# Reordering the per-chunk schedule of a fused phase mixer and ternary FFN layer, with the ternary comparisons on GpSimd

## The chip, the cores and the metric

The kernel runs on one core of a Trainium2 chip. The metric is the device time of one execution in microseconds; lower is better. Times inside an execution come from one profiled execution, counted from the start of its span.

## The reference

The input x is 16 sequences of 1024 positions and 256 features. Two residual layers follow each other, each on a layer norm of its input.

```python
omega = x @ W_omega.T + b_omega                       # x here: the layer norm of the input
phi = cumsum(omega * exp(log_scale) / sqrt(position), axis=1)
cm_real, cm_imag = x * cos(phi), x * sin(phi)
mem_real, mem_imag = (cumsum(c, axis=1) / position for c in (cm_real, cm_imag))
ret_real = mem_real * cos(phi) + mem_imag * sin(phi)
ret_imag = mem_imag * cos(phi) - mem_real * sin(phi)
h = layernorm(concatenate([cm_real, cm_imag, ret_real, ret_imag])) * gamma + beta
x = x + (gelu(h @ W1.T + b1) @ W2.T + b2)              # added to the mixer's own input and to x
# second layer: weights are ternary, clip(round(W / (mean|W| + EPS)), -1, 1)
out = x + (relu(layernorm(x) @ Wq1.T + b1) @ Wq2.T + b2)
```

## The kernel before, in words

The 16384 rows are cut into 32 chunks of 512; two chunks make a sequence, and the second takes over the running sums of the first. Each engine's stream is written out by hand: a start that works on chunks 0 and 1 and on the weights, and then a function `step`, called once per step s, which works on several chunks at once: `before` (s-1), `now` (s), `nxt` (s+1), `ahead` (s+2) and `far` (s+3). Semaphores carry the dependences (`need` and its kin wait for a chunk's count); within an engine the order is that of the calls, and a waiting instruction holds back all behind it.

What a chunk goes through: `statistics_1` and `normalise_1` (first layer norm), a split of the result in two float16 halves (`first_rows_hi`, `first_rows_lo`), which SP's DMA queue transposes into `turned1`; `omega` (TensorE, L908, 12 matmuls); `phase_turns` (L1193) and the scans `phase_sums` (L1202) on VectorE; `whole_turns` (ScalarE, L608) and `fraction` (L1213) reduce the phase; `sine`, `cosine`; `modulate_imag` and `modulate_real`, the scans `sums_imag` and `sums_real`, division by the position (`memory_imag`, `memory_real`, L1258), the four products of the retrieval, of which `product_imag_sin` (L550) is GpSimd's, and two accumulating DMAs from GpSimd's queue (`retrieve`). Each of the four context parts is split in halves (`context_hi` on ScalarE, `context_lo`, L1291, on VectorE). GpSimd adds the squares (`square_sums`, L534 and L536), and ScalarE takes them over with `sums_hi` (L652). TensorE then makes four hidden blocks (`hidden`, L948, 24 matmuls each) with `context_stats` and `spread` between them; the reciprocal deviations come back by `spread_out` (L662), and `scale_hidden` (L1315), `gelu`, `gelu_hi`, `gelu_lo` follow. `mixer_out` (L999, 48 matmuls) and `mixer_residual` (L1327) end the first layer.

Second layer: `statistics_2`, `spread_2`, GpSimd's `inverse_std_2` (L502), `lean_2`, `normalise_2` (L601), `second_hi`, `second_lo` (L1351); four DMA transposes from SP's queue (L441) give `turned2`. Then eight blocks: `ffn_in(m)` (L965, 4 matmuls of 512 columns), `relu` (L700) and `relu_hi` (L709) on ScalarE, `relu_lo` (L1359) on VectorE, and `ffn_out(m)` (L978, 8 matmuls of 256 columns), which runs three blocks behind. TensorE's order in a step is: hidden 0 and 1, context_stats, hidden 2, spread, hidden 3 (all for `nxt`), the eight input blocks and output blocks 0 to 4 (for `now`), mixer_out (`nxt`), omega (`far`), output blocks 5 to 7 (`now`). `last_mixer` holds the step in which chunk 30 goes through the FFN and chunk 31 through the mixer.

The ternary weights are made at the start. `signs` writes for each of the two matrices two float16 planes, weight above the threshold (L1500) and below its negative (L1501), 128x2048 elements each; TensorE turns them (`turn_signs`), and ScalarE copies them out. VectorE does `signs(0)` and `signs(1)` in step -1. The thresholds (`thr`, L1593 to L1595) are ready late in the part before the steps.

Quoted, the second layer's end of one block and the lag:

```python
for m in range(KF):
    if now:
        ffn_in(now, m, nxt)
        if m >= LAG:
            ffn_out(now, m - LAG)
```

## Time and profile before

| what | value |
| --- | --- |
| median of 3 runs | 1552.74 us (1551.18 to 1555.45) |
| the profiled execution | 1552.36 us, its span 1550.6 us |
| TensorE (PE) busy | 1480.5 us, 95% |
| VectorE (DVE) busy | 1395.3 us, 90% |
| ScalarE (ACT) busy | 1252.0 us, 81% |
| GpSimd (POOL) busy | 583.3 us, 38% |
| DMA | 158.73 MB, mean 102 GB/s |
| mean granted TensorE clock | 0.99 of full speed |

Busy time is a union over an engine's instructions; matmuls overlap each other, and their ends are modelled. The time outside the span, 1.8 us here, belongs to the execution but to no instruction. In the views, "idle before" is the time an engine stood still in front of an instruction, and the arrow names what ended it. PEq, DVEq, ACTq and SPq are the engines' sequencers.

### The profile page before, as it was taken

How to read it: one execution, taken by the hardware profiler on the slowest of the kernel's cores; microseconds unless marked ns; L12 is line 12 of the kernel's file. 1: busy time of each engine (PE TensorE's matmuls, PEld its weight loads, DVE VectorE, ACT ScalarE, POOL GpSimd, SP SyncE). 2: the span in 40 equal slices, each digit the busy share in tenths (PEclk: the TensorE clock that was granted, in tenths of full speed). 3: DMA queues.
4: the chain of work that ended last, by engine and by line, in shares of the span. 5: the costliest groups of instructions: out<-in, count | busy, mean ns of one | idle time of the engine just before them, and what ended most of it. 6: DMA issues, size and time to landing. Idle time of an engine off the chain costs nothing.

```text
span 1550.6 us, 29919 instructions
## 1 busy us (share of the span) xinstructions
PE 1480.5 (95%) x10677; PEld 875.2 (56%) x10677; DVE 1395.3 (90%) x2324; ACT 1252.0 (81%) x1773; POOL 583.3 (38%) x394
## 2 busy tenths in 40 slices
PE   3689999999999999999999999999999999999997
PEld 2355555656555655555565655566555556565564
DVE  6999999999999999999999999999999999999843
ACT  6768888888987888888888897888888888889755
POOL 1323344433344443334443334444333444333421
PEclk9799999999999999999999999999999999999999
DMA  6335655555765645675555567454566555556533
GB/s 217 68 56 110 123 93 100 101 96 104 123 114 88 103 95 94 122 123 93 99 103 96 103 123 119 82 107 95 93 120 123 95 97 103 98 101 109 96 55 55
DMA packets 233603, 158.73 MB, mean 102 GB/s; under 512 B 140784, under 2 KB 223728, under 8 KB 233456
## 3 DMA queue, kind: packets, MB, share of 16 engines
q0 software_dynamic: 59376, 83.37, 34.9%
q1 hardware_dynamic: 172448, 69.77, 19.6%
q10 hardware_dynamic: 1632, 3.67, 0.6%
q8 instruction: 86, 1.41, 0.4%
q14 instruction: 61, 0.50, 0.1%
HBM read 24.13 MB, written 33.03 MB: 37 GB/s over the span
## 4 chain that ended last, share of the span: by engine, by line
PE 47%; DVE 30%; issue 9%; ACT 5%; SPq 4%; DMA 4%; DVEq 0%; ACTq 0%; POOL 0%; POOLq 0%
PE ps L978 11%; PE ps L948 11%; PE ps L999 10%; PE ps L965 8%; PE ps L908 5%; SPq L441 4%; DVE ph L1202 3%; DVE mi L1234 3%; DMA turned<-rows 2%; DVE mr L1246 2%; DVE bn L1334 2%; DVE xs L1179 2%; DVE mi L1265 2%; DVE rows L1351 2%; DVE arena L1315 2%
## 5 line engine op out<-in xcount | busy, mean ns | idle before, releaser
L948 PE MATMUL ps<-arena,w_hi 128*128 128x512 f16 x2048 | 609.0, 379 | 1.8 <-DVE arena L1291 1.1
L948 PE MATMUL ps<-arena,w_lo 128*128 128x512 f16 x1024 | 388.0, 379 | 0.0
L948 PEld LDWEIGHTS ps<-arena,w_hi 128*128 128x128 f16 x2048 | 197.8, 98 | 223.3 <-issue 2.0
L978 PE MATMUL ps<-fw_t,arena 128*128 128x256 f16 x2048 | 254.6, 272 | 11.9 <-DVE arena L1359 10.9
L965 PE MATMUL ps<-turned,fw_t 128*128 128x512 f16 x1024 | 249.1, 381 | 11.5 <-DMA turned<-rows 11.1
L978 PEld LDWEIGHTS ps<-fw_t,arena 128*128 128x128 f16 x2048 | 193.7, 97 | 94.0 <-issue 39.3
L700 ACT ACTIVATE arena<-ps,relu_bias,relu_scale 128x512 f32<-128x512 f32 x256 | 191.8, 773 | 49.0 <-PE ps L965 49.0
L534 POOL TENSOR_TENSOR sqr<-sqr,turn 128x1024 f32<-128x1024 f32 x32 | 88.5, 2765 | 334.1 <-ACT sqr L648 320.5
L1359 DVE TENSOR_TENSOR arena<-arena 128x512 f16<-128x512 f32 x256 | 170.6, 686 | 20.6 <-ACT arena L709 19.8
L999 PE MATMUL ps<-w_hi,arena 128*128 128x256 f16 x1024 | 173.2, 273 | 0.3 <-issue 0.3
L948 PEld LDWEIGHTS ps<-arena,w_lo 128*128 128x128 f16 x1024 | 100.1, 98 | 120.8
L965 PEld LDWEIGHTS ps<-turned,fw_t 128*128 128x128 f16 x1024 | 98.3, 98 | 112.7 <-DMA turned<-rows 25.0
L709 ACT CAST arena<-arena 128x512 f16<-128x512 f32 x256 | 148.6, 616 | 1.5
L999 PE MATMUL ps<-w_lo,arena 128*128 128x256 f16 x512 | 139.7, 273 | 0.0
L550 POOL TENSOR_TENSOR qa<-mi,sn 128x1024 f32<-128x1024 f32 x32 | 76.5, 2390 | 96.6 <-DVE mr L1246 86.8
L999 PEld LDWEIGHTS ps<-w_hi,arena 128*128 128x128 f16 x1024 | 100.3, 98 | 12.4 <-issue 0.7
L666 ACT ACTIVATE arena<-arena,b_full,z_down 128x512 f32<-128x512 f32 x128 | 100.4, 808 | 1.7 <-DVE arena L1315 1.3
L1320 DVE SCALAR_TENSOR_TENSOR arena<-arena,up 128x512 f16<-128x512 f32 x128 | 94.8, 744 | 0.0
L502 POOL TENSOR_TENSOR rs<-ve,minus_half 128x4 f32<-128x4 f32 x32 | 59.7, 1867 | 91.3 <-DVE ve L1345 90.5
L483 POOL DMA_DIRECT2D rr<-qa x32 | 29.8, 931 | 169.1 <-DVE rr L1281 169.1
L652 ACT CAST sqr<-sqr 128x512 f16<-128x512 f32 x32 | 19.8, 618 | 90.8 <-POOL sqr L536 90.8
L1315 DVE TENSOR_TENSOR arena<-ps,rb 128x512 f32<-128x512 f32 x128 | 82.1, 683 | 10.9 <-ACT rb L662 6.5
(184 smaller groups left out, 2783.7 us busy)
## 6 DMA issues: line engine op xcount, KB each, us to landing
x_rows<-in_L_attn_x SPq DMA_DIRECT2D x32, 512.0 KB, 4.2
rr<-qa POOLq DMA_DIRECT2D x32, 512.0 KB, 5.0
ri<-qb POOLq DMA_DIRECT2D x32, 512.0 KB, 7.1
base<-bias_rows POOLq DMA_DIRECT2D x32, 512.0 KB, 6.0
x<-bias_rows POOLq DMA_DIRECT2D x32, 512.0 KB, 8.7
out<-x SPq DMA_DIRECT2D x31, 512.0 KB, 5.5
out<-x POOLq DMA_DIRECT2D x31, 512.0 KB, 6.1
arena<-in_L_attn_W ACTq DMA_DIRECT2D x1, 2048.0 KB, 11.7
```

Source lines behind the costliest of these rows:

```text
L534: pool.tensor_tensor(sqr[:, :, :], sqr[:, :, :], turn[:, :, :], ALU.add).then_inc(q2_done, 1)
L666: act.activation(z[:, m], z[:, m], ACT.Gelu, scale=z_down[:, 0:1], bias=b1_full[:, m:m + 1])\
L700: act.activation(rf[:, m % SLOTS], ps[:, 4 + m % KE], ACT.Relu, scale=relu_scale[:, 0:1], bias=relu_bias[:, m:m + 1]).then_inc(relu_done, 1)
L709: act.copy(rh[:, m % SLOTS], rf[:, m % SLOTS]).then_inc(rh_done, 1)
L908: last = pe.matmul(ps[:, 2 + e], w[:, k, e * P:(e + 1) * P], a[:, k], start=(i == 0), stop=(i == len(passes) - 1))
L948: last = pe.matmul(ps[:, 4 + m], w[:, k, m * P:(m + 1) * P], a[:, c.b, k], start=(i == 0), stop=(i == len(passes) - 1))
L965: last = pe.matmul(ps[:, 4 + m % KE], fw1_t[:, k, m * P:(m + 1) * P], a[:, k], start=(i == 0), stop=(i == len(passes) - 1))
L978: last = pe.matmul(ps_rows_a[:, j], a[:, m % SLOTS, j * P:(j + 1) * P], fw2_t[:, m], start=(m == 0 and j % 2 == 0 and a is rh), stop=(m == ...
L999: last = pe.matmul(rows[:, j], a[:, m, j * P:(j + 1) * P], w[:, m], start=(i == 0), stop=(i == len(passes) - 1))
L1315: dve.tensor_tensor(z[:, m], ps[:, 4 + m], rb[:, :], ALU.mult).then_inc(z_done[m], 1)
L1320: dve.scalar_tensor_tensor(out=gl[:, m], in0=z[:, m], scalar=up[:, 3:4], in1=gh[:, m], op0=ALU.mult, op1=ALU.subtract).then_inc(gl_done[m], 1)
L1359: dve.tensor_tensor(rl[:, m % SLOTS], rf[:, m % SLOTS], rh[:, m % SLOTS], ALU.subtract)\
```

## The change

On every engine the calls in `step` are put in another order. On TensorE omega(far) moves from behind mixer_out to between ffn_in(5) and ffn_out(2). On SP the transposes of `turned2` come before the load of `x_rows`. On ScalarE base_scaled comes ahead of whole_turns and output; cosine's absolute value becomes a call of its own; relu_hi(m) mostly follows relu(m). On VectorE lean_2 comes behind statistics_1, second_lo before memory_imag, the copies of the carries apart from their scans, phase_turns between context_lo 1 and 2, and phase_sums before statistics_2. On GpSimd base_bias comes first and output_sum behind retrieve. `signs` goes to GpSimd: its first pair ahead of the first square_sums, its second in step -1 ahead of retrieve. For the last chunk the rows `xs2` are transposed by TensorE as they are, behind ffn_out(5) of chunk 30, and split from PSUM by ScalarE and VectorE.

```diff
             def step(s):
-                if c := s.chunk(4):
-                    need(sp, scaled_done, c, 2)
-                    sp.dma_start(x_rows[:, c.b], x_v[c.index]).then_inc(x_loaded[c.b], 16)
-                if c := s.chunk(0):
+                if (c := s.chunk(0)) and c.index < CHUNKS - 1:
...
+                if c := s.chunk(4):
+                    need(sp, scaled_done, c, 2)
+                    sp.dma_start(x_rows[:, c.b], x_v[c.index]).then_inc(x_loaded[c.b], 16)
@@ gpsimd, step
+                if ahead:
+                    base_bias(ahead)
                 if now:
                     inverse_std_2(now)
-                if before:
-                    output_sum(before)
...
-                if ahead:
-                    base_bias(ahead)
...
                 if ahead:
                     product_imag_sin(ahead)
+                if nxt and not now:
+                    pool.wait_ge(p_fw2, 16)
+                    pool.wait_ge(p_tern, 2)
+                    signs(1, fw2_in, fw2_signs)
+                if ahead:
                     retrieve(ahead)
+                if before:
+                    output_sum(before)
+                if ahead:
                     square_sums(ahead)
...
+            def signs(i, w, into):
+                flat = w.rearrange("p m d -> p (m d)")
+                over, under = (into[:, s].rearrange("p m d -> p (m d)") for s in range(2))
+                pool.tensor_scalar(over, flat, thr[:, i:i + 1], None, ALU.is_gt).then_inc(p_tern, 1)
+                pool.tensor_scalar(under, flat, neg_thr[:, i:i + 1], None, ALU.is_lt).then_inc(p_tern, 1)
...
             retrieve(first)
+            pool.wait_ge(p_thr, 1)
+            pool.wait_ge(p_fw1, 16)
+            pool.wait_ge(p_turned, 1 + KC)
+            signs(0, fw1_in, fw1_signs)
             square_sums(first)
@@ scalar, last_mixer
                     if m == KF - 2:
                         normalise_2(last)
-                        second_hi(last)
                     relu(now, m)
                     relu_hi(now, m)
+                act.wait_ge(t1_done, 3)
+                need_block(act, f1_done, KF - 1, now)
+                act.copy(h2, ps[:, 2:4]).then_inc(h2_done, 1)
@@ scalar, step
                 if nxt:
                     sums_hi(nxt)
+                if ahead:
+                    base_scaled(ahead)
+                    whole_turns(ahead)
                 if before:
                     output(before)
                 if ahead:
-                    whole_turns(ahead)
-                    base_scaled(ahead)
                     sine(ahead)
+                    magnitude(ahead)
...
                 if now:
                     relu(now, 0)
+                    relu_hi(now, 0)
                 if nxt:
                     gelu_hi(nxt, 2)
...
-                    relu_hi(now, 0)
                     relu(now, 1)
+                    relu_hi(now, 1)
                     relu(now, 2)
-                    relu_hi(now, 1)
+                if ahead:
+                    square_real(ahead)
+                if now:
                     relu_hi(now, 2)
@@ tensor
+            def last_transposes(c):
+                need(pe, xs2_done, c)
+                need(pe, x1_done, c)
+                for k in range(KD):
+                    for j in range(NT):
+                        last = pe.transpose(ps[:, 2 + k, j * P:(j + 1) * P], xs2[:, j, k * P:(k + 1) * P], ident[:, :])
+                last.then_inc(t1_done, 1)
...
                     for m in range(KF - LAG, KF):
                         ffn_out(now, m)
+                        if nxt and m == KF - 3:
+                            last_transposes(nxt)
...
                     if now:
                         ffn_in(now, m, nxt)
-                        if m >= LAG:
-                            ffn_out(now, m - LAG)
+                    if m == 5 and far:
+                        omega(far)
+                    if now and m >= LAG:
+                        ffn_out(now, m - LAG)
...
                     mixer_out(nxt, now)
-                if far:
-                    omega(far)
@@ vector, last_mixer
-                    if m == 6:
-                        second_lo(last)
                     relu_lo(now, m)
+                need(dve, h2_done, last)
+                dve.tensor_tensor(l2, ps[:, 2:4], h2, ALU.subtract).then_inc(l2_done, 1)
```

VectorE's new order in a step is: fraction, statistics_1, lean_2, modulate_imag, sums_imag, gains_1, modulate_real, carry_imag, context_variance, second_lo, memory_imag, sums_real, unit_squares, carry_real, scale_hidden 0 to 2, first_rows_lo, memory_real, retrieve_imag_cos, scale_hidden 3, relu_lo 0, retrieve_real_cos, product_real_sin, relu_lo 1, context_lo 0, gelu_lo 0, relu_lo 2, first_join, gelu_lo 1, relu_lo 3, gelu_lo 2 and 3, relu_lo 4, context_lo 1, phase_turns, context_lo 2, relu_lo 5 and 6, context_lo 3, relu_lo 7, mixer_residual, phase_sums, carry_phase, statistics_2, spread_2.

## Rows read from the trace of the kernel before

**Rows 1.** Chain that ended last, longest pieces in order of time: start, us, what

```profile
146.60 5.24 PE ps L999 x48
...
1428.32 5.24 PE ps L999 x48
...
1438.78 10.36 PE ps L948 x48
...
1456.55 5.20 PE ps L948 x24
...
1469.15 0.87 PE ps L978 x8
```

**Rows 2.** Waits from 190 to 1430 us: us in total, times, longest

```profile
DVE ph L1193 <- PE ps L908: 33.3, 27, 1.3
DVE ph L1213 <- ACT turn L608: 25.3, 27, 1.2
PE ps L965 <- DMA turned<-rows: 6.2, 14, 0.9
```

**Rows 3.** Timeline of TensorE in one period: start, us, instruction

```profile
614.50 0.59 PE L948 MATMUL ps<-arena,w_hi 128*128 128x512 f16 x2
...
637.64 3.63 PE L965 MATMUL ps<-turned,fw_t 128*128 128x512 f16 x16
641.63 1.03 PE L978 MATMUL ps<-fw_t,arena 128*128 128x256 f16 x8 [0.36 <-DVE arena L1359]
...
643.37 1.03 PE L978 MATMUL ps<-fw_t,arena 128*128 128x256 f16 x8
```

**Rows 4.** Timeline of VectorE in the same period

```profile
615.40 2.46 DVE L1202 TENSOR_TENSOR_SCAN ph<-ones,ph_carry,ph 128x512 f32<-128x512 f32 x2
...
633.15 1.89 DVE L1315 TENSOR_TENSOR arena<-ps,rb 128x512 f32<-128x512 f32 x3
...
639.67 1.22 DVE L1281 TENSOR_TENSOR rr<-mr,cs 128x1024 f32<-128x1024 f32 x1
640.80 0.68 DVE L1359 TENSOR_TENSOR arena<-arena 128x512 f16<-128x512 f32 x1
...
642.54 1.28 DVE L1359 TENSOR_TENSOR arena<-arena 128x512 f16<-128x512 f32 x2
```

**Rows 5.** Timeline of ScalarE in the same period

```profile
638.72 0.78 ACT L700 ACTIVATE arena<-ps,relu_bias,relu_scale 128x512 f32<-128x512 f32 x1 [0.90 <-PE ps L965]
```

**Rows 6.** Costliest groups on the page: busy, mean ns of one, idle before

```profile
L709 ACT CAST arena<-arena 128x512 f16<-128x512 f32 x256 | 148.6, 616 | 1.5
```

**Rows 7.** Timeline of VectorE in the start

```profile
50.14 3.25 DVE L1281 TENSOR_TENSOR rr<-mr,cs 128x1024 f32<-128x1024 f32 x1
...
65.69 4.39 DVE L1202 TENSOR_TENSOR_SCAN ph<-ones,ph_carry,ph 128x512 f32<-128x512 f32 x2
...
75.74 1.28 DVE L1501 TENSOR_SCALAR x<-arena,neg_thr 128x2048 f16<-128x2048 f32 x1
```

**Rows 8.** Timeline of GpSimd in the start

```profile
0.74 0.20 POOL L468 MEMSET ident<- 128x128 f32 x1 [0.29 <-POOLq L1616]
1.19 0.29 POOL L470 TENSOR_SCALAR_AFFINE_SELECT ident<-ident 128x128 f32<-128x128 f32 x1 [0.24 <-POOL ident L468]
1.44 0.10 POOL L472 MEMSET e_base<- 128x2 f32 x1
...
49.05 3.26 POOL L550 TENSOR_TENSOR qa<-mi,sn 128x1024 f32<-128x1024 f32 x1 [9.78 <-DVE mi L1265]
```

**Rows 9.** Chain that ended last, at the last chunk

```profile
1530.54 5.31 PE ps L965 x16
```

**Rows 10.** Timeline of TensorE at the last chunk

```profile
1530.54 0.92 PE L965 MATMUL ps<-turned,fw_t 128*128 128x512 f16 x3 [3.95 <-DMA turned<-rows]
```

**Rows 11.** Timelines of ScalarE and VectorE at the last chunk

```profile
1518.88 2.08 ACT L601 ACTIVATE xs<-x,lean,rs 128x256 f32<-128x256 f32 x4 [0.30 <-DVE lean L1151]
...
1524.72 0.69 DVE L1359 TENSOR_TENSOR arena<-arena 128x512 f16<-128x512 f32 x1 [0.64 <-ACT arena L709]
```

More of the change, by code:

```diff
@@ L760, in step @@
                     second_hi(now)
+                if far:
+                    normalise_1(far)
                 if ahead:
@@ L864, in _ @@
             sine(first)
+            magnitude(first)
             cosine(first)
@@ L1405, in step @@
                     statistics_1(far)
-                if nxt and not now:
-                    dve.wait_ge(p_fw1, 16)
-                    signs(0, fw1_in, fw1_signs)
+                if now:
+                    lean_2(now)
                 if ahead:
@@ L1422, in step @@
                 if ahead:
+                    memory_imag(ahead)
                     sums_real(ahead)
+                if far:
+                    unit_squares(far)
+                if ahead:
+                    carry_real(ahead)
                 if nxt:
@@ L1448, in step @@
                     relu_lo(now, 1)
-                    relu_lo(now, 2)
+                if ahead:
+                    context_lo(ahead, 0, cmr[:, :, :])
                 if nxt and now:
                     gelu_lo(nxt, 0)
-                if ahead:
-                    context_lo(ahead, 0, cmr[:, :, :])
+                if now:
+                    relu_lo(now, 2)
+                if far:
+                    first_join(far)
                 if nxt and now:
@@ L1459, in step @@
                     gelu_lo(nxt, 2)
+                    gelu_lo(nxt, 3)
                 if now:
                     relu_lo(now, 4)
-                if nxt and now:
-                    gelu_lo(nxt, 3)
+                if ahead:
+                    context_lo(ahead, 1, cmi[:, :, :])
+                if far:
+                    phase_turns(far)
+                if ahead:
+                    context_lo(ahead, 2, rr[:, :, :])
                 if now:
                     relu_lo(now, 5)
-                if far:
-                    first_join(far)
+                    relu_lo(now, 6)
                 if ahead:
-                    context_lo(ahead, 1, cmi[:, :, :])
-                    context_lo(ahead, 2, rr[:, :, :])
                     context_lo(ahead, 3, ri[:, :, :])
                 if now:
-                    relu_lo(now, 6)
                     relu_lo(now, 7)
@@ L1479, in step @@
                 if far:
-                    phase_turns(far)
+                    phase_sums(far)
+                    carry_phase(far)
                 if nxt:
@@ L1483, in step @@
                     spread_2(nxt)
-                if far:
-                    phase_sums(far)
             def powers(cols):
@@ L1494, in powers @@
                 return dve.tensor_scalar(down[:, cols], pw[:, cols], 2.0 ** -14, None, ALU.mult)
-            def signs(i, w, into):
-                flat = w.rearrange("p m d -> p (m d)")
-                over, under = (into[:, s].rearrange("p m d -> p (m d)") for s in range(2))
-                dve.tensor_scalar(over, flat, thr[:, i:i + 1], None, ALU.is_gt).then_inc(p_tern, 1)
-                dve.tensor_scalar(under, flat, neg_thr[:, i:i + 1], None, ALU.is_lt).then_inc(p_tern, 1)
             first, second = first_chunks(dve)
@@ L1600, in _ @@
             phase_sums(second)
+            carry_phase(second)
             prepared(dve)
```

67 lines of the change are left out of this document (36 added, 31 removed).

## The prediction

> **What bounds the kernel now.** I read the profile from the end back to the engines. The chain of work, by its long pieces, shows one pattern from 146.60 to 1428.32 us: the second mixer product (L999) begins 28 times, so one chunk takes (1428.32 - 146.60) / 28 = 45.78 us [rows 1]. The pieces in one such period are nearly all TensorE. From one L999 to the end of the four hidden products (L948) is 1461.75 - 1428.32 = 33.43 us, of which the part from 1438.78 on is 22.97; the FFN adds eight input blocks (L965) and five output blocks (L978) of 0.87 each, 11.3 [rows 1]. That is 44.7 us without a gap: 1.1 us of a period is idle TensorE, 30 us over 28 periods. No reorder can take more than that from the middle.
>
> The waits over 27 of these periods say where VectorE idles: 33.3 us before L1193, on omega, and 25.3 before L1213, on ScalarE's whole turns [rows 2]. VectorE thus works 45.78 - 58.6/27 = 43.6 us of each: only 1.1 us lighter than TensorE. TensorE waits for relu_lo (L1359) in front of L978 [rows 3] and for the DMA transposes in front of L965, 6.2 us in 14 of the periods [rows 2].
>
> I then laid one period out from its first L948, at 614.50 = T 0 [rows 3]. ffn_in(0) begins at T 23.14, ffn_out(0) at 27.13 behind a wait of 0.36 for relu_lo(0), ffn_out(1) at 28.87 [rows 3]. Without the gap they could begin at 22.97, 26.45 and 28.2. On VectorE scale_hidden(0) begins at T 18.65, relu_lo(0) at 26.30, after retrieve_real_cos, and relu_lo(1) at 28.04 [rows 4].
>
> **The change, part by part.**
> *The middle, TensorE.* omega(far), 12 matmuls, goes from behind mixer_out to before ffn_out(2). No matmul is added; the floor stays 44.7. The two VectorE waits of rows 2 should mostly go, as omega is then long done, but VectorE is not what ends the period, so their 2.2 us are worth nothing by themselves.
> *The middle, relu_lo.* ScalarE's relu(0) begins 1.08 after ffn_in(0) [rows 5, 3]; relu_hi(0) now follows it directly. From T 22.97: relu 24.05, relu_hi 24.7 to 25.35 (L709, 0.616 [rows 6]), relu_lo(0) 25.35, 0.95 earlier than now. But retrieve_real_cos and product_real_sin, 1.13 each by start-to-start [rows 4], now both stand between relu_lo(0) and relu_lo(1): 25.35 + 0.60 + 2.27 = 28.2, and done (0.68 [rows 4]) at 28.9. ffn_out(1) starts near 29.05 instead of 28.2: the stall moves by one block and 0.9 stays. Behind it omega's 2.6 us give both engines time, and I find no second wait: relu_lo(2) to (4) come 2 us ahead of their blocks. New period: 44.7 + 0.9 = 45.6, or -0.2 x 28 = **-5.6 us**. The bounds are the floor (-1.1 a period) and a stall in the first half as well (below).
> *The middle, first half.* second_lo moves ahead of memory_imag and sums_real, so SP's four transposes start some 2 us sooner, and the x_rows load is issued behind them, no longer ahead; I cost the load at nothing, since it serves a chunk four steps on. If the load's 512 KB delay the accumulating DMAs that ScalarE reads, there is about 2 us of cover. On POOL's queue base_bias goes first and output_sum last; both serve later steps, nothing. On ScalarE base_scaled now precedes whole_turns, 2 us, hidden by phase_sums, which VectorE does sooner; the six small copies of carries only change place.
> *The comparisons.* VectorE loses four of 1.20 (1.28 for a single one) [rows 7]. GpSimd does them in the start, where the chain is almost solid VectorE. No row has such an operation on GpSimd. From above: its two-input product of 1024 elements takes 3.26, of which 0.9 is wait, so 2.3 ns an element [rows 8], 4.7 us for 2048. From below: VectorE's 1.2. Nearest in kind is the one-input select of 128 elements, 0.29, of which a tiny memset shows 0.10 to be fixed: 1.5 ns, 3.0 us; a memset of the same size takes 0.20, so 0.8 ns, 1.6 us [rows 8]. I take the middle of the last two with a little over, 2.4 us, an estimate. The profile also shows the two engines shutting each other out: L1281 takes 3.25 where it takes 1.22 later [rows 7, 4], as the product L550 runs to 52.31 [rows 8]; the scans L1202 take 4.39 [rows 7], beside square_sums on GpSimd. When the first pair of comparisons can start (the thresholds are ready just ahead of context_lo 1), VectorE has context_lo and the scans queued, all with two inputs, so each comparison holds VectorE for its whole length; the second pair likewise meets memory_real and the retrievals. Behind the first pair wait square_sums and, through it, ScalarE's sums_hi, base_scaled and whole_turns; this I put at another 0.7. Behind the second wait the DMAs of retrieve. Start: 4 x (2.4 - 1.2) + 0.7 = **+5.5 us**.
> By the Trainium skill (GPSIMD Engine Reference, Engine selection) GpSimd handles one-input elementwise work at about line rate. At its stated 1.2 GHz that would be an estimate of 1.7 us per comparison; the start would then cost +2.7 and the whole come to 1543. No row here shows such an instruction; the select's row speaks for something slower.
> *The end.* For the last chunk second_hi, second_lo and four DMA transposes give way to eight TensorE transposes, one ScalarE copy and one VectorE subtraction. Now TensorE waits 3.95 before the last chunk's ffn_in [rows 10], and its first 16 matmuls then take 5.31 [rows 9], against 4 x 0.87 = 3.5 in the middle. New: normalise_2 ends at 1520.96 as before [rows 11]; the transposes fit behind ffn_out(5). Without second_hi (1.05, an estimate from twice L709 less its fixed part) relu_lo(7), now at 1524.72 [rows 11], starts at 1523.7. The copy h2 runs 1523.6 to 1524.6, the subtraction (1.2) to 1525.8, and ffn_in(0) begins at 1525.95, not 1530.54: -4.6. With TensorE idle under 1 us the clock should hold, another -1.8: **-6.4 us**. Bounds: -4 (clock falls all the same) and -7.
>
> Sum: 5.5 - 5.6 - 6.4 = -6.5. The profiled execution took 1552.36 us, so 1545.9; the median of the runs lies 0.4 above it: 1546.
>
> **The rivals.**
> *Floor reached.* relu_lo(1) is in time, because VectorE gets through the pair before it faster, or TensorE's gaps that I cannot see go too. Period 44.75, -28.8 in the middle: 1552.4 + 5.5 - 28.8 - 6.4 = 1523. For it: every other wait of rows 2 loses its cause. Against: the sum of durations above. Chance 0.17.
> *GpSimd compares at its two-input rate*, 4.7 us each: start 4 x 3.5 + 0.7 = +14.7, whole +2.7, 1555. For it: the only wide GpSimd arithmetic in the trace runs at that rate. Against: it reads twice as much per result. Chance 0.13.
> *Slower: VectorE becomes the bound of every period.* phase_sums now meets square_sums, because context_lo(3) comes some 2 us later and the scans directly follow mixer_residual. The row of 4.39 against 2.46 in the middle [rows 7, 4] shows up to 2 us lost to that. VectorE's 43.6 plus 1.5 to 2, plus waits that stay (the spread of the deviations, relu_hi(0)), would make 46.1: +0.35 x 28 = +9.8, whole +8.9, 1561. It decides from the point where scale_hidden(0) begins later than about T 19.2; my walk has it at 18.9, so the margin is 0.3 to 0.4 us. The Trainium skill (Perfetto Trace Analysis, Optimizing Scalar/DVE Operations) warns that offloading between these two engines might not help for such a lock; the collision in rows 7 and 8 agrees. Chance 0.20.
>
> **How the numbers follow.** The forecast has 0.50, with a range of its own from 1540 to 1552. A measurement here can tell about 0.3% from no change: 1548.1 and 1557.4 are the bounds. Faster: 0.35 of the forecast and the floor's 0.17, 0.52. Same: 0.15 of the forecast and 0.11 of the slow comparisons, 0.26. Slower: the bound by VectorE and the rest, 0.22. The range runs from 1529, halfway into the floor's case, to 1561.
>
> **What would show it.** L965's wait on DMA goes; L978 waits about 0.9 a period for relu_lo, at ffn_out(1); the waits before L1193 and L1213 shrink to a third or less; scans L1202 grow from 2.4 to about 4 in each period; the four comparisons take 2 to 3 us each and neighbouring VectorE operations double; VectorE's first L1327 comes some 5 us later; the last ffn_in follows its predecessor within 1 us. I am wrong if the period is under 45.2 or over 45.9, or if the first steps come no later.

## The result, and the profile after

The changed kernel takes 1560.8 us, median of 5 runs (1559.86 to 1562.57); the kernel before took 1552.29 us beside it (1551.18 to 1555.45). The ratio is 1.0064, with a 95% interval of 1.0052 to 1.0077: slower by 8.5 us, where 6.7 us less than the first median had been forecast. The profiled execution took 1562.57 us, its span 1560.7.

The page shows that this isn't a matter of busy time on TensorE. PE does its work in 8 us less than before (1472.6 against 1480.5), while VectorE and GpSimd have become busier.

```profile
span 1560.7 us, 29930 instructions
...
PE 1472.6 (94%) x10685; PEld 880.5 (56%) x10685; DVE 1420.7 (91%) x2320; ACT 1256.8 (81%) x1773; POOL 647.9 (42%) x398
```

VectorE gave away four instructions and is busy for 25 us more: an instruction that stands still beside another engine's counts as busy. Most of the 25 us is in the phase scans of the middle, a pair of which now takes 3.42 us, shown below, where it took 2.46 [rows 4].

Line numbers have moved: ffn_in is L999 (was L965), ffn_out L1012 (L978), mixer_out L1033 (L999), omega L938 (L908), relu_lo L1409 (L1359), mixer_residual L1377 (L1327), the phase scans L1246 (L1202). The chain of the changed kernel gives the same marks as [rows 1]: the first, second and 30th mixer product (start, us, what).

```profile
118.62 5.33 PE ps L1033 x48
...
165.30 5.24 PE ps L1033 x48
...
1446.38 5.24 PE ps L1033 x48
```

They cut the time in three, and every later run is cut in the same way:

| stretch of the profiled execution | before | after | difference | predicted |
| --- | --- | --- | --- | --- |
| start, up to the second mixer product | 146.6 | 165.3 | +18.7 | +5.5 |
| middle, 28 periods | 1281.7 (45.78 each) | 1281.1 (45.75) | -0.6 | -5.6 |
| end, from the 30th product on | 122.3 | 114.3 | -8.0 | -6.4 |
| span | 1550.6 | 1560.7 | +10.1 | -6.5 |

**The start.** The timeline of GpSimd in the changed kernel has the operation that no row of before had:

```profile
60.87 7.40 POOL L562 TENSOR_SCALAR x<-arena,thr 128x2048 f16<-128x2048 f32 x1 [3.96 <-DVE thr L1642]
68.27 5.44 POOL L563 TENSOR_SCALAR x<-arena,neg_thr 128x2048 f16<-128x2048 f32 x1
73.69 2.69 POOL L540 TENSOR_TENSOR sqr<-sqr,turn 128x1024 f32<-128x1024 f32 x1
...
96.56 5.44 POOL L562 TENSOR_SCALAR arena<-arena,thr 128x2048 f16<-128x2048 f32 x1
102.00 6.85 POOL L563 TENSOR_SCALAR arena<-arena,neg_thr 128x2048 f16<-128x2048 f32 x1
108.81 0.94 POOL L483 DMA_DIRECT2D rr<-qa  x1
```

Two comparisons take 5.44 us, the others 6.85 and 7.40: more than twice the 2.4 of the forecast, above even its upper bound of 4.7. All four run beside busy VectorE work, so 5.44 is the shortest seen here and not a length measured alone. In the same stretch VectorE's timeline has

```profile
62.94 4.68 DVE L1341 TENSOR_TENSOR arena<-ri,arena 128x1024 f16<-128x1024 f32 x1
...
68.97 5.26 DVE L1246 TENSOR_TENSOR_SCAN ph<-ones,ph_carry,ph 128x512 f32<-128x512 f32 x2
...
81.61 1.23 DVE L1259 SCALAR_TENSOR_TENSOR ph<-turn,ph 128x1024 f32<-128x1024 f32 x1 [7.37 <-ACT turn L625]
...
97.05 4.31 DVE L1223 TENSOR_TENSOR xs<-qb,xs 128x1024 f16<-128x1024 f32 x1
...
104.15 4.05 DVE L1331 TENSOR_TENSOR rr<-mr,cs 128x1024 f32<-128x1024 f32 x1
```

Beside three of the comparisons one VectorE operation of 1.2 us is stretched to 4.05 to 4.68 us; beside the second one the two scans take 5.26 us, against 4.39 before [rows 7]. In the two longer comparisons VectorE still finishes operations of ordinary length for some 2 us after the comparison has begun, and only then is one of them stretched. The fraction (L1259) then waits 7.37 us for ScalarE's whole turns. ScalarE is late because sums_hi (L673) stands ahead of them and waits for square_sums, which in GpSimd's queue stands behind the first pair; base_scaled, which the change put ahead of the whole turns, adds two microseconds:

```profile
77.83 0.62 ACT L673 CAST sqr<-sqr 128x512 f16<-128x512 f32 x1 [13.65 <-POOL sqr L542]
78.36 2.07 ACT L598 ACTIVATE base<-x_rows,shift,gain 128x256 f32<-128x256 f32 x4
80.33 1.13 ACT L625 ACTIVATE turn<-ph,rounder 128x1024 f32<-128x1024 f32 x1
```

And TensorE's timeline shows a wait that the prediction does not mention: in step -1 omega(far) now stands ahead of the turning of the ternary weights, and waits for chunk 2's DMA transposes.

```profile
108.01 1.89 PE L938 MATMUL ps<-turned,wo_hi 128*128 128x512 f16 x4 [8.30 <-DMA turned<-xs]
```

The wait has a second price. The chain shows omega's 12 matmuls of this step and those of a later one:

```profile
108.01 5.30 PE ps L938 x12
...
158.37 2.59 PE ps L938 x12
```

The first take twice as long, with a granted clock of 0.50 from 104 to 113 us. The xs that the third comparison stretches (L1223, 4.31 us) is what chunk 2's transposes wait for, so this comparison reaches TensorE as well.

**The middle.** The waits from 190 to 1430 us (us in total, times, longest):

```profile
DVE x L1377 <- PE ps L1033: 27.1, 27, 1.0
PE ps L1012 <- DVE arena L1409: 23.9, 27, 0.9
DVE arena L1409 <- ACT arena L730: 15.1, 26, 1.0
DVE ph L1259 <- ACT turn L625: 8.7, 15, 0.6
PE ps L999 <- DMA turned<-rows: 0.4, 1, 0.4
```

Against [rows 2]: the wait on omega (33.3 us) is gone, the one on whole turns has shrunk from 25.3 to 8.7, TensorE's wait for the DMA transposes from 6.2 to 0.4. In their place stands one wait of 0.89 us in every period, of TensorE for relu_lo (L1409); before, TensorE's waits for relu_lo came to 7.4 us over the same stretch. One period of TensorE and, under it, of VectorE shows where; hidden(0) begins near 630.8 here.

```profile
653.76 3.62 PE L999 MATMUL ps<-turned,fw_t 128*128 128x512 f16 x16
657.21 1.04 PE L1012 MATMUL ps<-fw_t,arena 128*128 128x256 f16 x8
658.08 1.03 PE L999 MATMUL ps<-turned,fw_t 128*128 128x512 f16 x4
659.99 1.03 PE L1012 MATMUL ps<-fw_t,arena 128*128 128x256 f16 x8 [0.89 <-DVE arena L1409]
660.86 1.03 PE L999 MATMUL ps<-turned,fw_t 128*128 128x512 f16 x4
661.73 1.03 PE L938 MATMUL ps<-turned,wo_hi 128*128 128x512 f16 x4
```

```profile
629.58 3.42 DVE L1246 TENSOR_TENSOR_SCAN ph<-ones,ph_carry,ph 128x512 f32<-128x512 f32 x2
...
656.28 0.69 DVE L1409 TENSOR_TENSOR arena<-arena 128x512 f16<-128x512 f32 x1 [0.46 <-ACT arena L730]
...
659.16 0.69 DVE L1409 TENSOR_TENSOR arena<-arena 128x512 f16<-128x512 f32 x1
```

ffn_out(0) begins without a wait, ffn_out(1) at T 29.2 behind relu_lo(1). Counted from start to start the stall is longer than the idle time shown: the input block ahead of it takes 659.99 - 658.08 = 1.91 us, the next one 661.73 - 660.86 = 0.87, so 1.04 us are lost.

One thing changed in the middle that costs little here and comes back in the last experiments: on the page the two accumulating DMAs of retrieve take longer to land, `rr` 7.7 us (5.0 before) and `ri` 9.1 (7.1), and so does output_sum's, 12.1 (6.1). ScalarE waits for `ri` for 3.1 us in all.

**The end.** Before the last chunk's ffn_in TensorE waited 3.95 us [rows 10] and then took 5.31 for 16 matmuls [rows 9]. Now it waits 0.37 and takes 3.61, and the granted clock, 0.50 from 1531.5 to 1534.2 us before, stays at 1.00:

```profile
1538.66 1.04 PE L1042 MATMUL ps<-ident,xs 128*128 128x128 f32 x8
...
1542.38 3.61 PE L999 MATMUL ps<-turned,fw_t 128*128 128x512 f16 x16 [0.37 <-issue]
```

### The profile page after: what moved, and what is told of

Same layout as the page of the kernel before. It is cut to its first block, busy times and chain, and to the rows that moved or that the text cites. A ratio compares the mean times of both kernels' runs of the same rounds, so it can differ in the third digit from the quotient of the medians.

```text
span 1560.7 us, 29930 instructions
## 1 busy us (share of the span) xinstructions
PE 1472.6 (94%) x10685; PEld 880.5 (56%) x10685; DVE 1420.7 (91%) x2320; ACT 1256.8 (81%) x1773; POOL 647.9 (42%) x398
## 4 chain that ended last, share of the span: by engine, by line
PE 78%; DVE 8%; issue 5%; ACT 5%; POOL 2%; DMA 1%; SPq 1%; DVEq 0%; ACTq 0%; POOLq 0%
PE ps L978 39%; PE ps L1012 12%; PE ps L1033 10%; PE ps L999 7%; PE ps L938 5%; PE ps L951 3%; DVE rr L1331 2%; DVE arena L1409 2%; ACT arena L721 2%; ACT arena L730 1%; DMA arena<-in_L_attn_ln_beta 1%; PE ps L964 1%; POOL sqr L540 0%; POOL x L562 0%; DVE qb L1325 0%
## 5 line engine op out<-in xcount | busy, mean ns | idle before, releaser
L978 PE MATMUL ps<-arena,w_hi 128*128 128x512 f16 x2048 | 611.7, 380 | 6.6 <-DVE arena L1341 4.8
L978 PE MATMUL ps<-arena,w_lo 128*128 128x512 f16 x1024 | 389.3, 380 | 0.0
L978 PEld LDWEIGHTS ps<-arena,w_hi 128*128 128x128 f16 x2048 | 198.4, 98 | 229.4 <-issue 8.7
L1012 PE MATMUL ps<-fw_t,arena 128*128 128x256 f16 x2048 | 254.8, 272 | 27.2 <-DVE arena L1409 27.2
L1012 PEld LDWEIGHTS ps<-fw_t,arena 128*128 128x128 f16 x2048 | 197.9, 98 | 92.0 <-issue 46.5
L999 PE MATMUL ps<-turned,fw_t 128*128 128x512 f16 x1024 | 247.3, 379 | 1.4 <-DVE arena L1365 0.6
L721 ACT ACTIVATE arena<-ps,relu_bias,relu_scale 128x512 f32<-128x512 f32 x256 | 197.4, 771 | 35.4 <-PE ps L999 35.2
L540 POOL TENSOR_TENSOR sqr<-sqr,turn 128x1024 f32<-128x1024 f32 x32 | 84.0, 2626 | 331.4 <-DVE arena L1341 331.4
L1409 DVE TENSOR_TENSOR arena<-arena 128x512 f16<-128x512 f32 x256 | 172.9, 685 | 30.1 <-ACT arena L730 30.0
L1033 PE MATMUL ps<-w_hi,arena 128*128 128x256 f16 x1024 | 172.9, 273 | 0.3 <-issue 0.3
L978 PEld LDWEIGHTS ps<-arena,w_lo 128*128 128x128 f16 x1024 | 100.4, 98 | 121.8 <-issue 1.7
L730 ACT CAST arena<-arena 128x512 f16<-128x512 f32 x256 | 154.4, 615 | 4.3
L999 PEld LDWEIGHTS ps<-turned,fw_t 128*128 128x128 f16 x1024 | 99.7, 98 | 95.9 <-DMA turned<-rows 2.3
L673 ACT CAST sqr<-sqr 128x512 f16<-128x512 f32 x32 | 19.8, 618 | 157.2 <-POOL sqr L542 157.2
L1033 PE MATMUL ps<-w_lo,arena 128*128 128x256 f16 x512 | 139.6, 273 | 0.0
L1033 PEld LDWEIGHTS ps<-w_hi,arena 128*128 128x128 f16 x1024 | 100.2, 98 | 12.4 <-issue 0.7
L687 ACT ACTIVATE arena<-arena,b_full,z_down 128x512 f32<-128x512 f32 x128 | 96.9, 804 | 5.8 <-DVE arena L1365 5.4
L938 PE MATMUL ps<-turned,wo_hi 128*128 128x512 f16 x256 | 70.9, 402 | 20.2 <-DVE turned L1219 11.9
## 6 DMA issues: line engine op xcount, KB each, us to landing
out<-x POOLq DMA_DIRECT2D x31, 512.0 KB, 12.1
```

The source lines that it names most:

```text
L540: pool.tensor_tensor(sqr[:, :, :], sqr[:, :, :], turn[:, :, :], ALU.add).then_inc(q2_done, 1)
L687: act.activation(z[:, m], z[:, m], ACT.Gelu, scale=z_down[:, 0:1], bias=b1_full[:, m:m + 1])\
L721: act.activation(rf[:, m % SLOTS], ps[:, 4 + m % KE], ACT.Relu, scale=relu_scale[:, 0:1], bias=relu_bias[:, m:m + 1]).then_inc(relu_done, 1)
L730: act.copy(rh[:, m % SLOTS], rf[:, m % SLOTS]).then_inc(rh_done, 1)
L938: last = pe.matmul(ps[:, 2 + e], w[:, k, e * P:(e + 1) * P], a[:, k], start=(i == 0), stop=(i == len(passes) - 1))
L978: last = pe.matmul(ps[:, 4 + m], w[:, k, m * P:(m + 1) * P], a[:, c.b, k], start=(i == 0), stop=(i == len(passes) - 1))
```

## Experiments

The theory, formed on this profile: the loss is all in the start, and has two causes, the comparisons on GpSimd (slow themselves, and VectorE held for as long) and the new order in step -1 (omega ahead of turn_signs); the end brings 8 us; the middle keeps one stall. The rivals: the order costs nothing and the comparisons are the whole loss; or the loss lies only in what is queued behind the comparisons on GpSimd. "Start" below is the second mixer product in each profile.

### The comparisons back on VectorE

The changed kernel with `signs` on VectorE, as before (`signs(0)` behind statistics_1, `signs(1)` ahead of gelu_lo, both in step -1):

```diff
@@ gpsimd
-                if nxt and not now:
-                    pool.wait_ge(p_fw2, 16)
-                    pool.wait_ge(p_tern, 2)
-                    signs(1, fw2_in, fw2_signs)
...
-            pool.wait_ge(p_thr, 1)
-            pool.wait_ge(p_fw1, 16)
-            pool.wait_ge(p_turned, 1 + KC)
-            signs(0, fw1_in, fw1_signs)
@@ vector, step
                 if far:
                     statistics_1(far)
+                if nxt and not now:
+                    dve.wait_ge(p_fw1, 16)
+                    signs(0, fw1_in, fw1_signs)
...
                 if nxt and not now:
+                    dve.wait_ge(p_fw2, 16)
+                    dve.wait_ge(p_tern, 2)
+                    signs(1, fw2_in, fw2_signs)
                     for m in range(KE):
                         gelu_lo(nxt, m)
```

> The changed kernel with the four comparisons back on VectorE, at the places that they have in the kernel before. Theory A (the comparisons are the whole loss: 5.4 us each on GpSimd, with VectorE locked out or waiting behind them): the first L1033 comes at about 101 to 103 us instead of 118.6, the period stays 45.75, the end stays 8 us shorter, and the time is 1560.8 - 17 = 1544 (1542 to 1547). Rival B (the new order of the first steps is at fault, the comparisons cost 4 x 2.4 = 10 us at most): 1550 or more.

Measured: 1550.92 us, ratio 0.9992 (0.9983 to 1.0002). Start 153.68, middle 1280.7, end 114.3. This is rival B's time and not theory A's 1544. The comparisons account for 9.9 us of the changed kernel's time, but the start is still 7.1 us later than before (146.6): the new order alone costs that much, and eats nearly all that the end brings. A difference between two starts is good to about 1 us: the context_lo that stands ahead of any comparison begins at anything from 59.46 to 60.84 us in the profiles of this document. Counted from there, the order costs 8.2 us and the comparisons 10.7. Its TensorE timeline has the same wait for chunk 2's transposes, with GpSimd doing no comparison at all, and omega's 12 matmuls take 4.34 us behind it:

```profile
97.62 1.89 PE L923 MATMUL ps<-turned,wo_hi 128*128 128x512 f16 x4 [6.72 <-DMA turned<-xs]
```

### One pair at a time

The changed kernel with the second pair alone back on VectorE (the first pair on GpSimd), and with the first pair alone back.

> The changed kernel with only the second pair back on VectorE. Theory A with both pairs alike: half of the loss, 1552 (1550 to 1555). If what counts is ScalarE's wait for square_sums behind the first pair (whole_turns late by 10 us), then nearly all of the loss stays: 1557 or more.

> The changed kernel with only the first pair back on VectorE. Theory A with both pairs alike: 1552 (1550 to 1555). If the first pair's queue is what counts: 1547 or less. The second pair ends at 109 in the changed kernel, with the accumulating DMAs of retrieve behind it, so I expect at least 6 us of loss from it, 1550.

Measured: first pair on GpSimd 1559.52 us, ratio 1.0053 (1.0037 to 1.0068), start 163.16; second pair on GpSimd 1551.17, ratio 0.9993 (0.9984 to 1.0003), start 155.32. Against 153.68 with neither, the first pair costs 9.5 us of the start and the second 1.6 (8.6 and 0.3 in the medians). An instruction of the same form costs a sixth where it stands second. The expected 6 us of loss from the second pair did not come. Its time is near the 1550 forecast only by chance, as the kernel without any comparison on GpSimd had been put at 1544 and came out at 1551. VectorE's timeline says why the second pair costs so little. With both pairs on VectorE, its context_lo of step -1 waits 5.42 us for ScalarE, which copies the turned weights behind TensorE's wait for the transposes:

```profile
110.52 1.22 DVE L1326 TENSOR_TENSOR arena<-rr,arena 128x1024 f16<-128x1024 f32 x1 [5.42 <-ACT arena L635]
```

With the second pair on GpSimd (7.47 and 6.40 us here) the same instruction begins only 0.65 later, and the wait is 0.81:

```profile
111.17 1.22 DVE L1337 TENSOR_TENSOR arena<-rr,arena 128x1024 f16<-128x1024 f32 x1 [0.81 <-ACT arena L646]
```

Of the 5.42 us of idle time 4.6 are used up: there the time that VectorE lost to the pair went. The 0.65 are no cost of the pair either, as this profile is 0.74 later already at the context_lo ahead of any comparison.

### The comparisons alone, on the kernel before

```diff
@@ vector, step
-                if nxt and not now:
-                    dve.wait_ge(p_fw1, 16)
-                    signs(0, fw1_in, fw1_signs)
...
-                    dve.wait_ge(p_fw2, 16)
-                    dve.wait_ge(p_tern, 2)
-                    signs(1, fw2_in, fw2_signs)
@@ gpsimd
                     product_imag_sin(ahead)
+                if nxt and not now:
+                    pool.wait_ge(p_fw2, 16)
+                    pool.wait_ge(p_tern, 2)
+                    signs(1, fw2_in, fw2_signs)
+                if ahead:
                     retrieve(ahead)
...
             retrieve(first)
+            pool.wait_ge(p_thr, 1)
+            pool.wait_ge(p_fw1, 16)
+            pool.wait_ge(p_turned, 1 + KC)
+            signs(0, fw1_in, fw1_signs)
             square_sums(first)
```

> The kernel before with nothing changed but the engine of the comparisons, at the changed kernel's places in GpSimd's stream. Theory A: the loss does not need the new order; the start is 15 to 19 us longer, 1552.3 + 17 = 1569 (1567 to 1572). Rival B: 1562 or less, as here whole_turns is not behind base_scaled and VectorE's order is the old one.

Measured: 1560.17 us, ratio 1.0058 (1.0041 to 1.0075). Start 156.47, 9.9 more than before; middle 1278.7; end 122.4, as before. The move of the comparisons costs the old order 9.9 us of the start against the new one's 11.6, far less than theory A's 15 to 19. The middle is 3.0 us shorter than in the profile of the kernel before, which this edit does not explain.

### The first pair behind the work that queued behind it

The changed kernel, `signs(0)` behind `square_sums(first)` and `base_bias(first)`:

```diff
             retrieve(first)
+            square_sums(first)
+            pool.wait_ge(p_bias, 32)
+            base_bias(first)
             pool.wait_ge(p_thr, 1)
             pool.wait_ge(p_fw1, 16)
             pool.wait_ge(p_turned, 1 + KC)
             signs(0, fw1_in, fw1_signs)
-            square_sums(first)
-            pool.wait_ge(p_bias, 32)
-            base_bias(first)
```

> The changed kernel with the first pair of comparisons behind square_sums and base_bias on GpSimd's queue, so that ScalarE's sums_hi and whole_turns no longer wait for them; the comparisons then run beside fraction, statistics and the first modulations. If the 9.5 us of the first pair are the queue (whole_turns 10 us late): at least 6 us come back, 1554 or less. If they are mostly VectorE locked out for the length of each comparison: VectorE meets them later instead, with the scans of chunk 1, and less than 3 us come back, 1558 or more.

Measured: 1558.66 us, ratio 1.0037 (1.0017 to 1.0058), start 162.05. The queue ahead of whole_turns is gone (the fraction waits 2.81 us, as in the first experiment), and 2.1 us come back (3.3 in the start) of some 9.5: most of the price stays. The pair now stands at 68.91 and 74.45 and takes 5.96 and 5.83. VectorE meets it at other operations, both of 1.2 us in the first experiment:

```profile
72.00 2.22 DVE L1259 SCALAR_TENSOR_TENSOR ph<-turn,ph 128x1024 f32<-128x1024 f32 x1 [2.81 <-ACT turn L625]
...
78.50 4.30 DVE L1272 TENSOR_TENSOR cmi<-xf,sn 128x1024 f32<-128x1024 f32 x1
```

These two hold 4.1 us. What else the pair costs there is not taken apart: GpSimd's work of step -1 still stands behind it (square_lo begins at 80.69 against 73.09).

### What sets the length of a comparison

The changed kernel with other operations on the same tiles: the first pair is a comparison with a constant and a product with a constant, the second a copy with the cast to float16 and a product with a per-partition scalar. The weights are then not the ternary ones; nothing else is changed. It was profiled in one execution, for the lengths alone.

```diff
+                if i == 0:
+                    pool.tensor_scalar(over, flat, 0.015, None, ALU.is_gt).then_inc(p_tern, 1)
+                    pool.tensor_scalar(under, flat, 2.0, None, ALU.mult).then_inc(p_tern, 1)
+                else:
+                    pool.tensor_copy(over, flat).then_inc(p_tern, 1)
+                    pool.tensor_scalar(under, flat, neg_thr[:, i:i + 1], None, ALU.mult).then_inc(p_tern, 1)
+                return
```

> The changed kernel, where the four comparisons on GpSimd are replaced by four other operations on the same tiles, so its weights are not the ternary ones: greater than an immediate, times an immediate, a plain copy with the cast to float16, and times a pointer scalar. Only their durations count, to set beside 5.44 us for a comparison with a pointer scalar. If the comparison itself is the cost: the product and the copy take 3 us or less and the comparison with an immediate 5.4. If the pointer scalar is the cost: the immediates take 3 us or less and the pointer product 5.4. If it is the size and the cast: all four take about 5.4.

Its GpSimd timeline:

```profile
60.06 6.28 POOL L563 TENSOR_SCALAR x<-arena 128x2048 f16<-128x2048 f32 x1 [3.94 <-DVE thr L1652]
66.33 5.72 POOL L564 TENSOR_SCALAR x<-arena 128x2048 f16<-128x2048 f32 x1
...
94.86 1.89 POOL L566 CAST arena<-arena 128x2048 f16<-128x2048 f32 x1
96.75 7.45 POOL L567 TENSOR_SCALAR arena<-arena,neg_thr 128x2048 f16<-128x2048 f32 x1
```

In their places the comparisons of the changed kernel took 7.40, 5.44, 5.44 and 6.85 us. A product thus takes about what a comparison takes, and a constant about what a per-partition scalar takes, to within the us or so that the meetings with VectorE add; the copy of the same 2048 elements, cast included, takes 1.89, a third. It is the tensor-with-scalar instruction that is slow on GpSimd, 2.7 ns an element against 0.92, not the comparison, the operand or the cast.

### omega behind the turning of the weights

On the kernel of the first experiment; only step -1 changes:

```diff
-                    if m == 5 and far:
+                    if m == 5 and now and far:
                         omega(far)
...
                         turn_signs(n)
+                    omega(far)
                 if nxt:
                     mixer_out(nxt, now)
```

> The first run's kernel (new order, comparisons on VectorE), with omega(2) of step -1 behind the turned ternary weights and ahead of mixer_out; all later steps as changed. Theory C (the 7.1 us that the new order costs in the start come from TensorE, which waits 6.7 us for chunk 2's DMA transposes with the weights' transposes queued behind, so that ScalarE and then VectorE run late): mixer_residual at about 108 to 109 instead of 112.8, the time 1550.9 - 5 = 1546 (1544 to 1547.5). Rival D (base_scaled ahead of whole_turns, and phase_sums against square_sums, cost them): 1550 or more.

Measured: 1546.34 us, ratio 0.9963 (0.9953 to 0.9973), 4.6 us less than without the edit; start 150.32. So half of what the order costs in the start, 3.4 of 7.1, is that one wait and the slow omega behind it. The same edit on the changed kernel itself:

> The changed kernel, comparisons on GpSimd, with omega(2) of step -1 behind the turned weights. If the two losses in the start are separate: -4.6 as with the comparisons on VectorE, 1556. If TensorE has to wait for the second pair anyway (it ends at 109, chunk 2's transposes land at 108): 0 to -3, 1558 to 1561. I expect the second, 1558.5.

Measured: 1556.74 us, ratio 1.0023 (1.0012 to 1.0033): 4.1 less than the changed kernel. Between these two kernels lie the comparisons alone, 10.4 us: the two losses add, which was not the expected case.

### The last chunk alone

The kernel before with nothing but the last chunk's transposes on TensorE (`last_transposes`, `h2`, `l2`; no DMA and no second_hi and second_lo for it).

> The kernel before with the last chunk's rows turned by TensorE, and nothing else. All of the end's gain is this part: -8 us, 1552.5 - 8 = 1544.5 (1543 to 1546). If part of the gain in the end came from the new order of the last full steps: -5 us or less, 1547.5 or more.

Measured: 1543.76 us, ratio 0.9950 (0.9934 to 0.9966). Start 145.7, middle 1280.5, end 115.8, or 6.5 less than before; the time fell by more, 9.4 against the median beside it. In the profiles the other 2 us of the difference lie in the start and the middle, which the edit does not touch, so 6.5 is what is shown for it; the remaining 1.5 of the changed kernel's 8.0 in the end came with the new order. Its TensorE timeline shows the term:

```profile
1520.96 1.03 PE L984 MATMUL ps<-fw_t,arena 128*128 128x256 f16 x8
1522.30 1.03 PE L984 MATMUL ps<-fw_t,arena 128*128 128x256 f16 x8 [0.30 <-DVE arena L1375]
1523.69 3.61 PE L971 MATMUL ps<-turned,fw_t 128*128 128x512 f16 x16 [0.36 <-issue]
```

Taken alone, this part of the change beats the kernel before by half a per cent.

### The stall of the middle

On the kernel with omega late, relu_lo(1) ahead of product_real_sin, so that only retrieve_real_cos stands between relu_lo(0) and relu_lo(1):

```diff
+                if now:
+                    relu_lo(now, 1)
                 if ahead:
                     product_real_sin(ahead)
-                if now:
-                    relu_lo(now, 1)
```

> As the run before, with relu_lo(1) ahead of product_real_sin on VectorE. Theory E (the one stall left in a period, 0.9 us before ffn_out(1), is the two products between relu_lo(0) and relu_lo(1)): relu_lo(1) comes 1.14 earlier, the stall goes, 28 periods of 44.85 instead of 45.75, -25 us: 1521 (1518 to 1526). Rival F (VectorE, with some 43.5 us of work in a period, or the DMA that waits for product_real_sin, takes the stall over): no more than -10 us, 1536 or above.

Measured: 1534.14 us, ratio 0.9898 (0.9864 to 0.9932), 12 us less than without it, half of what the 28 stalls of 0.89 hold (25), and between theory E's range and rival F's. Some 2.6 of the 12 are in the start (147.7 against 150.3 in the profiles). Its runs scatter from 1529.35 to 1543.61, and in the profile the undisturbed periods last 44.85 us, others up to 51.6. The waits from 190 to 1420 name what took the stall's place: ScalarE waits for the accumulating DMA of `ri`.

```profile
ACT arena L635 <- DMA ri<-qb: 29.6, 22, 2.3
```

The page gives the landing of two DMAs of this kernel (KB each, us from issue to landing):

```profile
x_rows<-in_L_attn_x SPq DMA_DIRECT2D x32, 512.0 KB, 6.5
...
ri<-qb POOLq DMA_DIRECT2D x32, 512.0 KB, 9.0
```

The change had put the load of `x_rows` behind the transposes, near that DMA. The next kernel is this one with the load back at the head of SP's step.

```diff
             def step(s):
+                if c := s.chunk(4):
+                    need(sp, scaled_done, c, 2)
+                    sp.dma_start(x_rows[:, c.b], x_v[c.index]).then_inc(x_loaded[c.b], 16)
                 if (c := s.chunk(0)) and c.index < CHUNKS - 1:
...
-                if c := s.chunk(4):
-                    need(sp, scaled_done, c, 2)
-                    sp.dma_start(x_rows[:, c.b], x_v[c.index]).then_inc(x_loaded[c.b], 16)
```

> The kernel of the relu_lo run with the load of x_rows back at the head of SP's step, ahead of the transposes. In that run ScalarE waited 29.6 us in 27 periods for the accumulating DMA of ri, and periods scattered from 44.85 to 51.6. Theory G (the load of 512 KB, issued at the same moment as rr, ri and the stores, delays ri): the waits for ri fall below 10 us, the periods come near 44.9, and the time is 1526 (1523 to 1530). Rival H (the load is not what delays ri): no difference from the relu_lo run, 1533 to 1535, with the same scatter.

Measured: 1532.31 us (1532.0 to 1534.77), ratio 0.9875 (0.9857 to 0.9893), the fastest of all kernels here, 1.25% under the kernel before. The same wait and the same two landings:

```profile
ACT arena L635 <- DMA ri<-qb: 7.7, 12, 1.1
```

```profile
x_rows<-in_L_attn_x SPq DMA_DIRECT2D x32, 512.0 KB, 4.0
...
ri<-qb POOLq DMA_DIRECT2D x32, 512.0 KB, 7.9
```

The wait fell by 22 us, the median by 1.8 only, short of theory G's 1526; the two ratios' intervals overlap, so a gain in time is not shown. The runs of this kernel lie within 2.8 us, where those of the kernel without the edit spread over 14; inside the profile the periods still vary, from 44.85 to 49.43 us. The profile's span is 11 us shorter, but the one of the kernel without the edit was taken of its slowest run, so the differences of waits and landings between these two pages are partly those of a slow run: the changed kernel itself, with the load at the same late place, landed `x_rows` after 4.7 us and `ri` after 9.1. Last, I put output_sum's DMA (`out<-x` on GpSimd's queue) ahead of x1_bias (`x<-bias_rows`), nearer to where the kernel before had it, to keep it clear of `ri`:

```diff
+                if before:
+                    output_sum(before)
                 if now:
                     x1_bias(now)
...
                     retrieve(ahead)
-                if before:
-                    output_sum(before)
```

> As the run before, with GpSimd's output_sum ahead of x1_bias instead of behind retrieve. If output_sum (read and write of 512 KB in DRAM, 12 us to landing now) is the greater part of the crowd at that moment: 1524 (1521 to 1528) and less scatter than the run before. If not: the same as the run before within 2 us.

Measured: 1541.34 us, ratio 0.9932 (0.9918 to 0.9946), 9 us slower than without it. TensorE's wait for the second layer's transposes is back:

```profile
PE ps L983 <- DMA turned<-rows: 16.3, 25, 1.3
```

It was 3.3 us in 5 of the periods in the kernel without this edit. ScalarE's wait for `ri` nearly went (0.8 us in all), and the page has

```profile
ri<-qb POOLq DMA_DIRECT2D x32, 512.0 KB, 6.3
...
x<-bias_rows POOLq DMA_DIRECT2D x32, 512.0 KB, 8.3
...
out<-x POOLq DMA_DIRECT2D x31, 512.0 KB, 6.3
```

against 7.9, 5.6 and 10.1 without the edit. So output_sum and `ri` land sooner apart from each other, but x1_bias, now issued right behind output_sum, lands later. The likely reading, from these rows alone, is that the two are still under way when the four transposes start; output_sum's place behind retrieve is the better one for the time.

## Why the prediction was wrong

The forecast named faster, and the time came out 0.64% slower, at the upper edge of the range.

In the terms of its sum, -6.5 became +10.1 in the span: the comparisons cost 6.1 more than forecast, the order in the start 7.1 where nothing had been put, the middle gave 5.0 less, and the end 1.6 more. Put right alone, either of the first two brings the forecast's sum to about nothing (-0.4 and +0.6); together, and with the middle, they make it a loss.

**The comparisons' length was one term that failed.** "I take the middle of the last two with a little over, 2.4 us": 5.44 was measured. The choice was made by kind: the select's row, 1.5 ns an element, and a memset. The two-input product, 2.3 ns [rows 8], was set aside as reading twice as much, and called the bound from above; the instruction turned out slower than that one too (2.7 ns), so the bound did not hold. An instruction of another form is no bound, in either direction. By the Trainium skill (GPSIMD Engine Reference, Engine selection) one-input work runs there at about line rate. The copy agrees, 1.89 us against the estimate of 1.7; the tensor-with-scalar form does not, so the rule holds here for one of the two forms.

**The formula would have been too large with the true length.** It held VectorE for each comparison's whole length: 4 x (5.44 - 1.2) + 0.7 = 17.7. The runs show 11.6 in the start (165.30 - 153.68). The first pair's 9.5 comes near two such terms and the queue (2 x 4.24 + 0.7 = 9.2), but by luck: with that pair alone on GpSimd, context_lo is held 3.5 us longer than in the first experiment (4.68 against 1.22) and the scans 0.9 (5.26 against 4.39), and the fraction waits 4.6 longer for whole_turns (7.38 against 2.81), less the 2.4 that VectorE no longer spends on the pair. So VectorE was held for about half of what the formula says, and the queue, put at 0.7, cost several times that. Without the queue the pair met other VectorE work, so only 2.1 came back in the time: the parts do not add. The second pair's 1.6 is small because 5.42 us of idle time stood behind it on VectorE. The prediction's "the second pair likewise" took the cost over without asking what comes next.

**The order's price in the start was missing.** The prediction walks omega's move through a period of the middle, and never through step -1, where `now` is empty: no ffn work lies ahead of omega there, so it comes early, meets transposes that haven't landed, and holds back turn_signs and the first mixer_out. That costs 7.1 us with the comparisons on VectorE, of which 3.4 in the start (4.6 in the time) were given back by moving the one call; the wait of 6.72 us and omega at the halved clock are both in them. The other 3.7 are not settled. Candidates that the rows suggest are base_scaled ahead of whole_turns, which the forecast costed at nothing under phase_sums (the fraction waits 2.81 us in the first experiment, 1.32 before), and the next scans beside square_sums (4.63 us in the first experiment, 2.33 before); neither was tried alone.

**The middle: the mechanism held, the stall was mis-sized.** The stall moved by one block as forecast, to ffn_out(1). The floor of 44.7 was right: most periods last 45.73 us (165.30 to the next mark, 211.03), and without the 1.04 that the stall takes from start to start 44.69 are left. But 0.9 had been put for the stall. relu_lo(0) began at T 25.5 and not at 25.35, so ffn_out(1) came at T 29.2 where 29.05 was worked out, and its place without a stall is T 28.15, not 28.2. An error of 0.14 us in 45 is most of the whole expected gain per period (0.2), times 28. Almost all of the 1.1 us of idle time a period that the forecast saw is thus still there. The shortest periods of the kernel that takes the stall away last 44.85, so 0.9 of it could be had by that.

**The end** was right in its mechanism: the wait went, and so did the fallen clock (16 matmuls in 3.61 us and not 5.31). It gave -8.0 against -6.4, beyond the bound of -7; the part alone gave -6.5 in its own end.

**The rivals.** The slow comparisons (1555) came nearest in mechanism, with a length of 4.7. With 5.44 its sum gives 1558, and with the missing 7.1 of the order 1565: beyond the result, because its formula is too large. The slower rival, 1561, gave the time and is refuted all the same: VectorE did not become the bound. The scans take 3.42 us beside GpSimd, not quite the 4 feared, VectorE waits 1.0 us in each period for mixer_out, and the period did not grow. The floor's rival needed relu_lo(1) in time, which the change does not bring; the kernel that brings it reaches 44.85 in some periods and has ScalarE waiting for `ri` in 22 of 27.

The point that decides between faster and slower was then a single one: 18.7 us in a start that runs once, against 8.6 us from all the rest.

## What to carry to other kernels

When a call moves in a function that every step shares, walk it through the first and the last step too, where half of the conditions are empty: there the work that covered its wait is missing. Before an instruction is given to another engine, time that very form there: the nearest row of another form missed by a factor of two, and the engine it left had operations of 1.2 us held for over 4. A stall is counted from start to start: the 0.89 us of idle time shown cost 1.04 in each period, and where the whole gain is 0.2 us in 45, such an error decides.

## What the hardware showed

- GpSimd takes 5.44 us at the shortest for a tensor-with-scalar comparison on 2048 float32 elements a partition, written as float16, and about the same for a product (5.72 with a constant); 1.89 for the copy with the same cast. VectorE takes 1.2 for the comparison [rows 7].
- While it runs, one VectorE operation with two tensor inputs stretches from 1.2 to 4.05 to 4.68 us, and some of the comparisons take 6.85 to 7.47: the meeting can cost both.
- After TensorE had waited 8.30 us, 12 matmuls took 5.30 us at a granted clock of 0.50, against 2.59 in the next step at 1.00.
- DMAs of 512 KB landed later where they were issued close together. With output_sum's right ahead of x1_bias's, x1_bias's took 8.3 us against 5.6, and TensorE's waits for the transposes that followed rose from 3.3 to 16.3 us; away from output_sum, `ri` landed after 6.3 us against 7.9, and output_sum's own after 6.3 against 10.1.
